# The second maxima of each head group, transposed one step later in the first attention

## What is computed

```python
q_blhd = jnp.einsum('bld,dhk->blhk', x_bld, Wq)
latent_bll = jnp.einsum('bld,dc->blc', x_bld, Wkv_down)
k_blhd = jnp.einsum('blc,chk->blhk', latent_bll, Wk_up)
v_blhd = jnp.einsum('blc,chk->blhk', latent_bll, Wv_up)
attn = jnp.einsum('bqhd,bkhd->bhqk', q_blhd, k_blhd) / jnp.sqrt(HD)
attn = jax.nn.softmax(jnp.where(mask, attn, neg_inf), axis=-1)
y_blhd = jnp.einsum('bhqk,bkhd->bqhd', attn, v_blhd)
return jnp.einsum('bqhd,hdo->bqo', y_blhd, Wout)
```

## Time and profile before

| what | value |
|---|---|
| time, median of 3 runs | 2133.75 us (2133.57 to 2134.24) |
| the profiled execution | 2139.04 us, its span 2137.3 us |
| PE busy in the span | 1855.7 us, 87% |
| DVE busy | 1659.7 us, 78% |
| ACT busy | 1123.6 us, 53% |
| POOL busy | 955.2 us, 45% |
| groups 1 to 7 of the first attention | from about 80 us to about 455 us of the span |

### The profile page before, as it was taken

One profiled execution on the slowest core, in us unless ns is written; L12 is line 12 of the kernel. 1 busy time (PEld: TensorE's weight loads), 2 busy tenths in 40 slices (PEclk: granted clock), 3 DMA queues, 4 the chain that ended last, 5 costly groups with the idle time before them and its releaser, 6 DMA issues.

```text
span 2137.3 us, 32729 instructions
## 1 busy us (share of the span) xinstructions
PE 1855.7 (87%) x12452; PEld 1203.5 (56%) x12452; DVE 1659.7 (78%) x2131; ACT 1123.6 (53%) x1868; POOL 955.2 (45%) x365
## 2 busy tenths in 40 slices
PE   6899998986888886799999978888888777899998
PEld 4444454455444446577777745555555455677776
DVE  4556555548799998667777599999999999876676
ACT  2344444443533323345555557776777666555554
POOL 3356555622366751101000078888989889400000
PEclk8799999998999998799999999999999999999999
DMA  3111212000200001001010000000001000000000
GB/s 84 31 31 31 53 25 45 2 12 1 50 0 1 0 1 35 20 14 32 30 30 16 1 1 2 1 2 2 2 1 31 2 2 1 31 30 30 15 15 21
DMA packets 35681, 39.14 MB, mean 18 GB/s; under 512 B 5891, under 2 KB 22534, under 8 KB 35526
## 3 DMA queue, kind: packets, MB, share of 16 engines
q1 hardware_dynamic: 34998, 36.01, 6.7%
q10 hardware_dynamic: 528, 1.05, 0.2%
HBM read 21.05 MB, written 1.05 MB: 10 GB/s over the span
## 4 chain that ended last, share of the span: by engine, by line
PE 50%; DVE 19%; issue 19%; POOL 7%; ACT 4%; DMA 1%; SPq 0%; DVEq 0%; ACTq 0%; POOLq 0%; PEldq 0%
PE ps L46 9%; PE ps L47 8%; PE ps L48 8%; DVE negm L2661 6%; PE ps L530 4%; PE ps L546 3%; PE ps L571 2%; PE ps L579 2%; DVE AF L2668 2%; POOL AF L1572 2%; POOL hc L1572 1%; POOL AR_plain L2466 1%; PE ps L2490 1%; PE ps L2573 1%; DVE AF L823 1%
## 5 line engine op out<-in xcount | busy, mean ns | idle before, releaser
L2661 DVE TENSOR_REDUCE negm<-ps 128x64 bf16<-128x1024 f32 x256 | 303.6, 1224 | 20.3 <-PE ps L2564 20.2
L2466 POOL TENSOR_TENSOR AR_plain<-AF 128x2048 f32<-128x2048 f32 x64 | 261.9, 4095 | 31.4 <-ACT AF L2617 31.3
L753 POOL TENSOR_TENSOR AF<-AF 128x2048 f32<-128x2048 f32 (+3 forms) x52 | 184.5, 3549 | 197.0 <-ACT AF L693 195.1
L46 PE MATMUL ps<-XH,AR 128*128 128x512 f32 x616 | 255.2, 414 | 14.7 <-DVE XL L251 4.0
L2625 ACT ACTIVATE AF<-ps 128x1024 f32<-128x1024 f32 x192 | 196.5, 1023 | 133.5 <-PE ps L2573 132.2
L48 PE MATMUL ps<-XH,AR 128*128 128x512 f32 x616 | 245.7, 399 | 0.0
L47 PE MATMUL ps<-XL,AR 128*128 128x512 f32 x616 | 245.5, 399 | 0.0
L693 ACT ACTIVATE AF<-ps 128x512 f32<-128x512 f32 (+1 forms) x304 | 155.1, 576 | 157.1 <-PE ps L533 72.0
L2573 PE MATMUL ps<-negm,ident_bf 128*128 128x512 bf16 x512 | 161.4, 398 | 80.7 <-DVE negm L2661 80.2
L2668 DVE TENSOR_REDUCE AF<-AF 128x128 f32<-128x2048 f32 x96 | 219.4, 2286 | 0.0
L285 POOL TENSOR_SCALAR var_eps<-mv 128x8 f32<-128x8 f32 x10 | 4.2, 423 | 371.1 <-DVE mv L262 371.0
(11 more groups left out here) (338 smaller groups left out, 4389.5 us busy)
## 6 DMA issues: line engine op xcount, KB each, us to landing
AR<-AR SPq DMA_DIRECT2D x96, 128.0 KB, 2.4
AF<-in_L_ffn_Wg_dram SPq DMA_DIRECT2D x21, 256.0 KB, 2.7
AF<-in_L_ffn_Wu_dram SPq DMA_DIRECT2D x21, 256.0 KB, 3.1
AF<-in_L_ffn_Wd_dram SPq DMA_DIRECT2D x21, 256.0 KB, 3.8
AF<-AF SPq DMA_DIRECT2D x16, 64.0 KB, 2.4
AF<-AR_plain SPq DMA_DIRECT2D x16, 64.0 KB, 2.4
AF<-in_L_attn_a_Wq_dram SPq DMA_DIRECT2D x1, 512.0 KB, 4.0
AF<-in_L_attn_a_Wout_dram SPq DMA_DIRECT2D x1, 512.0 KB, 8.9
```

Of the source, the lines that this page charges most:

```text
L46: pe.matmul(out, ah, bh, start=start, stop=False)
L753: pool.tensor_tensor(zacc[u % 2][:, :, c0:512], zacc[u % 2][:, :, c0:512], pt[t % 4][:, :, 0:w], ALU.add).then_inc(s0_zp, 1)
L2466: pool.tensor_tensor(p6[m % 3].rearrange("p (j q i) -> p j q i", j=HJ, i=2), e6[m % 4].rearrange("p (j q i) -> p j q i", j=HJ, i=2), w6i[: ...
L2661: dve.tensor_reduce(negm6[:, j % 4, :], bank(2 * (j % 3), 2).rearrange("p (j q i) -> p q j i", j=HJ, i=2), mybir.AxisListType.XY, ALU.max, ...
```

## The change

The item `("n", gg, 1)` of the groups 1 to 7 moves from step A1 to step A2. There it is the only item. `parts` has a new rule for that case, by which it stands in the last third, behind the scores of A2 and the values of A1. The quotas are otherwise the same, the list of items has the same order, and no operation is added or taken away.

```diff
-        plan(diagonal(1, 0) + [("n", 1, 0)] + full(1) + diagonal(1, 1) + [("n", 1, 1)], range(4, 14),
-             (4, 4, 4, 4, 4, 5, 5, 5, 3, 2))
+        plan(diagonal(1, 0) + [("n", 1, 0)] + full(1) + diagonal(1, 1) + [("n", 1, 1)], range(4, 15),
+             (4, 4, 4, 4, 4, 5, 5, 5, 3, 1, 1))
         for gg in range(2, NG0):
             t0 = 12 * (gg - 1)
             plan([("q", gg, 0), ("q", gg, 1)], (t0 - 2, t0 - 1), (1, 1))
             plan(diagonal(gg, 0) + [("n", gg, 0)] + full(gg) + diagonal(gg, 1) + [("n", gg, 1)],
-                 range(t0 + 3, t0 + 14), (4, 4, 3, 3, 3, 3, 4, 4, 5, 5, 2))
+                 range(t0 + 3, t0 + 15), (4, 4, 3, 3, 3, 3, 4, 4, 5, 5, 1, 1))
...
         def parts(t):
 
             x = PLAN[t]
+            if len(x) == 1 and x[0][0] == "n":
+                return [], [], x
             k = (len(x) + 2) // 3
             return x[:k], x[k:2 * k], x[2 * k:]
```

## The result

The changed kernel took 2118.53 us (median of 6 runs, 2114.38 to 2121.68), against 2133.66 us for the kernel before on the same chips. The ratio is 0.9925 with a 95% interval from 0.9908 to 0.9943. By the ratio that is a saving of 16.0 us, between 12.2 and 19.6 us; the two medians are 15.1 us apart. The forecast was 19.2 us and 2114.6 us; the time lies in its range of 2109 to 2125 us. The profiled execution took 2121.68 us, its span 2119.9 us, 17.4 us less than that of before.

A forecast was written before the change was run, and what follows sets the result against it. PE, busy 87%, was taken as the bound, with 20.3 us of waits at the transposition and half-clock matmuls behind. 20.4 - 0.25 - 1.0 = 19.2 us saved from 2133.75 us gave 2114.6 us, range 2109 to 2125 us.

The forecast's parts named there:

- Where n stands: Start of the transposition of the second maxima (n) is not pushed back; idle ahead left as about 0.5 + 0.1 + 0.7 us.
- The scores of A3 and PE's own work: Behind the transposition, scores of A3 start at n + 0.31; 2.91 us of work makes PE ready for B0 at n + 3.22.
- The new bound: Scores of B0 wait for the DMAs of the maxima, landing at n + 3.55; each stretch shrinks to 3.55 us.
- second rival: Maxima land late in groups 1 to 6: stretch 5.25 us, saving 10.2 us less, time 2124.8 us; chance 0.06.
- The clock: PE stays at full clock around the transposition in groups 1 to 6; bounds of the cost 0 and 14.3 us.
- Group 7's clock: PE stands over a second us before B0 in group 7 and falls to half clock: 1.0 us allowed, bounds 0 and 2.7.
- POOL: Last addition of the A steps ends at n + 6.72: 0.66 us slack at `z` in B1, group 7 loses 0.25 us.
- The sum: Seven stretches from transposition to scores of B0 save 20.4 us; less 0.25 and 1.0 us, 19.2 us in all.

The follow-up runs named there:

- filled kernel: The kernel before with 11 useless matmuls just ahead of the transposition's wait in groups 1 to 7, order unchanged; 0.9942 of the kernel before, 12.4 us faster.

## Why the prediction was right, point by point

*Where n stands.* Right. The remaining wait is 0.58 us (0.7 foretold). The pieces ahead of it did not move n.

*The scores of A3 and PE's own work.* Right: n + 0.31. PE is ready at about n + 3.4 (3.22 foretold), since it waits only 0.17 us for the DMA in group 2 (0.33 foretold).

*The new bound.* Right, and its size too: 3.55 us from group 0 were 3.53 to 3.58 us in groups 1 to 5 and 3.48 us in group 7, but for 3.97 us in group 3 of the first trace. That it is the DMA was shown by cutting it. The one miss is group 6, with 4.2 to 4.5 us in both traces: the late landing of the second rival is real in one group of seven, 0.7 to 0.9 us in all and not 10.

*The clock.* Right. It was the one term of size that I had to choose, and it stayed up around n in all seven groups, in both traces. The filled kernel shows that this is 12.2 of the 19.1 us. The rule of the Trainium skill on frequent micro-idles (page "TensorE: Matmul & The Clock Gate", section "A second HAM failure mode: psum-queue depth-cycling") gives no size, and it did not hold for pieces of this size: the 0.28 and 0.58 us ahead of n and the 0.17 us behind it, in group 2, left the clock at 1.00, and so did those of the six other groups.

*Group 7's clock.* Mis-sized. I allowed 1.0 us for a fall behind the wait at B0. The wait was there, 1.87 us, but in the first trace the clock stayed at 1.00 behind it. In the second it did fall, to 0.64 over the 4.8 us behind B0, and still `z` stands at n + 6.98 in both, since POOL's last addition holds it. Neither trace shows a price of this fall.

*POOL.* Mis-sized, though little hung on it. I put the whole idle time between its first two additions (0.50 us in the earlier trace rows) down to the exponentials of A2 and let it go to nothing. In the traces of before it is 0.34 to 1.08 us in the seven groups. In those of the changed kernel it is 0.14 us in six groups, and in group 2 it did not shrink at all: the row has the same 0.50 us and names POOL itself as its releaser. So POOL keeps a time of its own between the two, as the second waits by a semaphore for the first. For group 3 the first two rows here are those of before; the third, of after, has both additions in one row, 5.96 us long:

```profile
221.13 3.44 POOL L753 TENSOR_TENSOR AF<-AF 128x1536 f32<-128x1536 f32 x1 [10.40 <-ACT AF L693]
225.21 2.35 POOL L753 TENSOR_TENSOR AF<-AF 128x1024 f32<-128x1024 f32 x1 [0.63 <-ACT AF L693]
...
216.26 5.96 POOL L755 TENSOR_TENSOR AF<-AF 128x1536 f32<-128x1536 f32 x2 [10.44 <-ACT AF L695]
```

The last addition ends at n + 6.83 to n + 6.90, in group 2 at n + 7.21, and not at n + 6.72. Why group 2 needs 0.50 us, in every trace here, stays open. The slack at `z` is 0.2 us in group 2 and 0.5 us in groups 1 and 5, in place of 0.66 us. In group 7 `z` waited 0.77 us where I had 0.25 us, but it stands at n + 6.98 and not far from the n + 6.74 that I had. The 2.94 us from B0 to `z`, which I took from the trace of before, began at half clock there. The kernel with the last `d` in A0 gained nothing because POOL's additions do not move with the transposition.

*The sum.* From the trace: 72.89 - 54.00 = 18.9 us up to the `z` products, and 72.0 - 53.3 = 18.7 us in the second pair of traces. That the first comes so near to 19.2 us is in part luck: the late DMAs of groups 3 and 6 took 1.4 us that I had not counted, and the 1.0 us for the clock of group 7 was not paid. The first row of DVE behind the attention stands 18.4 us earlier (461.33 and 442.90 us), and 16.0 us in the second pair (460.00 and 444.02 us).

Where the saving of the program fell short, the step that I had wrong is group 0, which I put at nothing because the change does not touch it. Its stretch to `z` was 9.43 and 9.42 us in the two traces of before, and 10.58 us in both of after. From its transposition to that of group 1 the rows are these, before, before again, after, and after again:

```profile
79.70:128.54 48.84, 43.26 (x265) 21.70 (x265) 27.89 (x47) 22.19 (x44) 23.16 (x8) 0.92 0.16 34
79.25:128.10 48.85, 43.27 (x264) 21.69 (x265) 27.88 (x47) 22.18 (x44) 23.15 (x8) 0.92 0.16 34
78.71:129.01 50.30, 46.23 (x276) 23.07 (x277) 27.88 (x47) 23.17 (x46) 23.15 (x8) 0.90 0.15 33
80.25:131.88 51.63, 47.83 (x276) 23.51 (x277) 27.89 (x47) 23.15 (x46) 23.05 (x8) 0.87 0.15 32
```

That is 1.5 us more in the first pair and 2.8 us in the second, at a lower granted clock. (PE is busy for longer in the rows of after also because the moved scores and values now run in them, within the old wait.) By (1 - PEclk) / 0.5 x length, as in the prediction, the half clock lasts 2.2 and 5.6 us longer, which at its 0.46 is an estimate of 1.0 and 2.6 us. Taken off 18.9 and 18.7 us, the 1.5 and 2.8 us leave 17.4 and 15.9 us, and the timed runs show 15 to 16 us. Why the clock stays low for longer there, in code that did not change, stays open. Behind the attention the two pairs differ by scatter: from that DVE row to the end of the span it is 1676.0 and 1676.6 us in the two traces of before, and 1677.0 and 1670.2 us in those of after.

## What to carry to other kernels

When TensorE waits with ready work queued behind the waiting instruction, count the wait and the matmuls at half clock behind it; here the second was the larger, 12.2 of 19.1 us. A filling of useless matmuls in the same place tells the two apart in one run. Before moving an instruction past others, look for the transfer that hangs on it: its landing is the new bound. A place in the same program where it is already waited for gave its length to 0.07 us in 11 of 14 stretches; the other three were 0.4 to 0.9 us longer. Measure the parts that the edit does not touch as well: here the clock of group 0 took back 1.5 to 2.8 us.

## What was not expected of the hardware

- One wait of 1.36 us ahead of the transposition, with another of 0.28 us before it, brought PE to 1.2 GHz in groups 1, 4 and 7 and left it at 2.4 GHz in groups 2, 3, 5 and 6. A wait of some 1.9 us at B0 in group 7 of the changed kernel left it at 2.4 GHz in one execution and not in the other (PEclk 0.64 over the 4.8 us behind it). A wait of 2.67 us brought it to 1.2 GHz in six groups of seven in both traces of before, and in five of seven with the DMAs cut. So the length of a wait alone does not decide. Yet the two executions of the kernel before had the same clock in groups 1 to 6.
- POOL needed 0.14 us from the end of its addition of 3.44 us to the start of the next, which waits for it by a semaphore, in groups 0, 1 and 3 to 7 of both traces of the changed kernel, and 0.50 us in group 2. In the kernel before, the profile named ACT for those 0.50 us.
- Two DMAs of 8 KB landed after 1.9 us, and after 2.4 to 2.5 us where a fetch of instructions was under way.
